# Attention with one reciprocal per group, its output and residual placed inside the next group's first pair, and the raw context copied by ScalarE

## The chip, the cores and the metric

The kernel runs on one core of a Trainium2 chip. The metric is the device time of one execution in microseconds (us). A core has TensorE (PE), VectorE (DVE), ScalarE (ACT), GpSimd (POOL) and SyncE (SP), which issues most of the DMAs. PSUM has eight banks of 128x512 f32.

## The reference

A decoder block on 32 sequences of 128 tokens with 128 features, in three stages with a layer norm behind each:

```
x = layernorm(x + mixer(x))              # a state-space scan
x = layernorm(x + attention(x, ctx))     # 16 heads of 8, mask, softmax, output weights
x = layernorm(x + experts(x))            # 16 experts, top 4, one shared expert
```

The change is in the second stage:

```
q, k, v = heads(x @ Wq + bq), heads(ctx @ Wk + bk), heads(ctx @ Wv + bv)
scores  = where(mask, -1e15, q @ k.T / sqrt(8))
attn    = softmax(scores);  out = (attn @ v) @ Wo + bo
```

## The kernel before, in words

`build` runs `mixer`, `attention` and `experts` one behind the other, each a block in which every engine has its own program, ordered against the others by semaphores. All sequences stand in SBUF as `x1` and `x2`.

`attention` (L949) works on eight groups of four sequences (`GS`, `NG`). The function `ahead` (L100) runs the same group function on each engine: a loop of two iterations of two groups, then four groups unrolled, whose argument `left` says how many groups follow. In group g the kernel finishes attention for g, takes the maxima of the scores for g+1, and makes q, k and v for g+2. Each sequence b of four is handled in two pairs p; a pair covers two banks.

- PE's `both(g, b, p)` (L1355) makes the transposed scores of g (`scoresT`, banks TT0 and TT1, read by ACT's exponentials at L1126) and the plain scores of g+1 (`scores`, banks SS0 and SS1, read by DVE's `maxima`, the reductions at L1211). Each `scores` waits until the reductions of the pair before have freed its banks. Both begin with the mask's product (L1328) and go on with the products at L1338. The first `scores` of a group waits in `stacked` (L1318) for `q_stack` and `k_stack` of g+1, first half.
- q and k of g+2 come from f32 products (`k_proj`, `q_proj`, L243), are split into three bf16 parts (ACT L208 and L214, DVE `part_rest` L221, POOL `part_third` L228), stored by SP to DRAM (`store_parts`, L253 and L256) and read back as stacks in two halves (`stack_k` L266, `stack_q` L275). `x1T` (L234) transposes x1 for q; DVE makes its low part at L201.
- The maxima of g+1 are split into bf16 parts by DVE (`split_maxima`, L1220 to L1226), transposed by PE (`max_rows`, L1387), copied by ACT (`store_max`, L1134), sent through DRAM (L1138) and laid under the q stack (`stack_max`, L1145). `scoresT` of a sequence waits for it.
- `weigh(b, 0)` (L1377) multiplies the probabilities with v, `weigh(b, 1)` with ones, so that the second half of the bank holds each head's row sum, already spread over the head's eight rows. DVE's `norm(b)` (L1228) takes the reciprocal of the 128x128 sums and multiplies, once for each sequence; the banks U0 and U1 alternate.
- `output(g)` (L1391) multiplies the four contexts with Wo into U0, and `residual_dve` (L114) adds `xb` (x1 and the bias, made by POOL at L1080) and takes the statistics for the layer norm; `normalise_pool` (L130) ends it on POOL.

The order on each engine is written out by hand. PE: pair 0 of sequence 0, k's product, the transposes of x1, pair 1, sequence 1 with q's product behind it, and so on; at the end `weigh(3, 1)`, v's product, `max_rows`, `output`. DVE: the reductions of sequence 0, x1's low part and k's rest, those of sequence 1, the split, q's rest, the others with `norm` between them, v, the residual. The last groups (`left` 1 and 0) hold the first steps of the experts' stage; POOL loads the experts' weights in the group with `left` 2 (L1523 and on).

Of the kernel before, what the change touches and what calls it, by code (L numbers as in the profile page):

```python
# [23 lines left out]
P = 128  # L24
# [924 lines left out]
def attention(nc, t, d, psum, a, e):  # L949
# [12 lines left out]
    with ExitStack() as ctx:  # L962
# [12 lines left out]
        ones_d = sb("ones_d", [P, UNITS * DIAG])  # L975
# [10 lines left out]
        recip = sb("recip", [P, 2, P])  # L986
# [13 lines left out]
        v_v, v_norm, v_max = sem("v_ready", GS), sem("ctx_norm", 2 * GS), sem("max_ready", 4 * GS)  # L1000
# [3 lines left out]
        p_mt, p_o = sem("max_mm", 2), sem("out_b_mm")  # L1004
# [16 lines left out]
        def _(sp):  # L1021
# [21 lines left out]
            def group(g, par, left):  # L1043
                if left == 3:
                    loads(g + 3, 1 - par)
# [14 lines left out]
        def _(pool):  # L1060
# [17 lines left out]
            def group(g, par, left):  # L1078
                pool.wait_ge(v_res.sem, v_res.at(g - 1, 0))
                pool.tensor_tensor(xb[:, :, :], x1[:, bass.ds(g * GS, GS), :], bc(b_o[:, None, :], [P, GS, P]), ALU.add)\  # L1080
                    .then_inc(g_x.sem, 1)
                if left >= 2:
                    masks(g + 2, par, (0,))
                    part_third(pool, a, g + 2, 1)
                    masks(g + 2, par, (1,))
                    part_third(pool, a, g + 2, 0)
                    masks(g + 2, par, (2, 3))
                if left == 3:
                    context_lo(g + 3, 1 - par)
# [15 lines left out]
            pool.memset(ones_d[:, :], 0.0).then_inc(g_init, 1)  # L1105
            normalise_pool(pool, NG - 1, t["x1_res"], x1_out, res, mv, rstd, norm_c, x1[:, NSEQ - GS:, :])
            pool.wait_ge(g_init, 6)
            pool.memset(ones_d[:, :].rearrange("p (i c) -> p i c", i=UNITS)[:, :, 0:P]
                        .rearrange("p i (c e) -> p i c e", e=4 * XD)[:, :, :, 0:XD], 1.0).then_inc(g_init, 1)
# [4 lines left out]
            prepare_pool(pool, e, prob[:, 0, 0:2, :, :].rearrange("p u i (x y) -> p (u i) x y", x=2))  # L1114
            ahead(pool, group)

        @block.scalar
        def _(act):
            for s in (a_exp, a_mt, *d_m, *d_ms, e.a_x, e.a_l, e.a_c):
                s.prime(act)  # L1120
# [27 lines left out]

            def group(g, par, left):
# [20 lines left out]
                exps(g, 2, 1)  # L1170
                if left:
# [5 lines left out]
                if left == 3:  # L1177
                    context_hi(act, a, g + 3, 1 - par)
# [13 lines left out]
        def _(dve):  # L1192
# [35 lines left out]
            def norm(g, b):  # L1228

                bank = (U0, U1)[b % 2]  # L1230
                dve.wait_ge(p_u.sem, p_u.at(g, b))
                dve.reciprocal(recip[:, b % 2, :], bank[:, P:2 * P]).then_inc(v_norm.sem, 1)  # L1232
                dve.wait_ge(v_norm.sem, v_norm.at(g, 2 * b))
                dve.wait_ge(p_o.sem, p_o.at(g - 1))
                dve.tensor_tensor(ctxT[:, b, :], bank[:, 0:P], recip[:, b % 2, :], ALU.mult).then_inc(v_norm.sem, 1)

            def group(g, par, left):
                if left:
                    maxima(g + 1, 0)
                if left >= 2:  # L1240
                    x1T_lo(dve, a, g + 2, PO)
                    part_rest(dve, a, g + 2, 1, PF)
                if left:
# [4 lines left out]
                if not left:  # L1248

                    dve.wait_ge(e.steps, PREPARED)  # L1250
                    x2T_lo(dve, e, 0, 0)
                if left:
                    maxima(g + 1, 2, (0, 1))
                norm(g, 0)
                if not left:
                    expert_scores(dve, e, 0)
                    rank_groups(dve, e, 0)
                if left:
                    maxima(g + 1, 2, (2, 3))
                    maxima(g + 1, 3, (0, 1))  # L1260
                norm(g, 1)
                if not left:
# [664 lines left out]
```

## Time and profile before

| what | us |
|---|---|
| median of 3 runs | 716.78 (712.73 to 718.43) |
| profiled execution | 715.72 |
| its span, first to last instruction | 713.9 |
| attention, about | 280 to 506 of the span |

How to read it: a row of a timeline is the start, the busy time of the merged instructions, the engine (q behind it: its sequencer, which issues DMAs), the line, the operation, out<-in, shapes and the number of instructions; in brackets the idle time of the engine just before and what ended it. Busy shares are means over stages with different limits.

### The profile page before, as it was taken

How to read it: one execution, taken by the hardware profiler on the slowest of the kernel's cores; microseconds unless marked ns; L12 is line 12 of the kernel's file. 1: busy time of each engine (PE TensorE's matmuls, PEld its weight loads, DVE VectorE, ACT ScalarE, POOL GpSimd, SP SyncE). 2: the span in 40 equal slices, each digit the busy share in tenths (PEclk: the TensorE clock that was granted, in tenths of full speed). 3: DMA queues.
4: the chain of work that ended last, by engine and by line, in shares of the span. 5: the costliest groups of instructions: out<-in, count | busy, mean ns of one | idle time of the engine just before them, and what ended most of it. 6: DMA issues, size and time to landing. Idle time of an engine off the chain costs nothing. (4 is left out here: it accounts for less than half of the span.)

```text
span 713.9 us, 17982 instructions
## 1 busy us (share of the span) xinstructions
PE 617.0 (86%) x6336; PEld 506.1 (71%) x6336; DVE 513.1 (72%) x1294; ACT 247.1 (35%) x428; POOL 259.7 (36%) x299
## 2 busy tenths in 40 slices
PE   6599999999998744978789879589799999999995
PEld 5468778778776532766567667467688888888884
DVE  3877887797785634778588888375477778787873
ACT  2453343354342301534436544234222222222221
POOL 4353854665564374342334435602101101110111
PEclk9989999999999955889799999688799999999998
DMA  6010000000000773276383565500000000000000
GB/s 200 5 56 2 15 15 15 0 15 15 0 16 1 172 165 67 82 131 149 80 180 117 120 140 144 120 7 4 30 1 30 30 0 29 29 0 29 16 16 16
DMA packets 53552, 40.32 MB, mean 56 GB/s; under 512 B 3968, under 2 KB 48288, under 8 KB 53488
## 3 DMA queue, kind: packets, MB, share of 16 engines
q1 hardware_dynamic: 50896, 36.74, 21.3%
q0 software_dynamic: 704, 1.92, 1.2%
q10 hardware_dynamic: 1888, 0.79, 0.5%
q8 instruction: 43, 0.70, 0.4%
q14 instruction: 21, 0.17, 0.1%
HBM read 24.10 MB, written 11.93 MB: 50 GB/s over the span
## 5 line engine op out<-in xcount | busy, mean ns | idle before, releaser
L1211 DVE TENSOR_REDUCE nmax<-bank 128x4 f32<-128x512 f32 x128 | 82.2, 684 | 56.2 <-PE bank L1338 55.9
L1824 PE MATMUL bank<-xT_hl_c,w_up 128*128 128x512 f32 x432 | 119.5, 413 | 1.9 <-ACTq L67 1.9
L133 POOL TENSOR_TENSOR rstd<-mv,norm_c 128x4 f32<-128x4 f32 x24 | 6.7, 281 | 306.7 <-DVE mv L127 285.9
L1126 ACT ACTIVATE prob<-bank 128x512 f32<-128x512 f32 x128 | 69.6, 596 | 99.7 <-PE bank L1338 87.2
L1328 PE MATMUL bank<-neg_i,mask 64*128 64x256 bf16 x512 | 58.4, 311 | 35.6 <-DVE nmax L1211 12.5
L1824 PEld LDWEIGHTS bank<-xT_hl_c,w_up 128*128 128x128 f32 x432 | 77.6, 193 | 15.7 <-ACTq L67 2.4
L1746 ACT ACTIVATE sg<-bank 128x512 f32<-128x512 f32 x72 | 43.1, 599 | 107.0 <-PE bank L1824 106.6
L1840 PEld LDWEIGHTS bank<-w_down,hid 128*128 128x128 f32 x576 | 74.4, 191 | 5.9 <-issue 0.6
L726 POOL TENSOR_TENSOR ramp<-upto,dec_hl 128x512 fp32r<-128x512 f32 x64 | 67.0, 1074 | 26.1 <-PE bank L856 26.1
L1840 PE MATMUL bank<-w_down,hid 128*128 128x128 f32 x576 | 75.6, 275 | 0.0
L1779 DVE TENSOR_TENSOR gu<-sg,bank 128x512 f32<-128x512 f32 x64 | 43.9, 685 | 21.8 <-PE bank L1824 10.3
L1328 PEld LDWEIGHTS bank<-neg_i,mask 64*128 64x128 bf16 x512 | 17.7, 101 | 53.9 <-issue 26.4
L1783 DVE TENSOR_TENSOR hid<-gu,bank 128x512 f32<-128x512 f32 x64 | 44.0, 688 | 6.5
L864 PE MATMUL bank<-w_x,xhl 128*128 128x256 f32 x192 | 42.2, 329 | 0.0
L1377 PE MATMUL bank<-prob,v_d 128*32 128x128 f32 x1024 | 38.6, 297 | 0.2 <-ACT prob L1126 0.2
L409 PE MATMUL bank<-xhl,w_feat 128*128 128x512 f32 (+1 forms) x96 | 30.2, 451 | 5.1 <-DVE b_rot L760 4.0
L1377 PE MATMUL bank<-prob,ones_d 128*32 128x128 f32 x1024 | 34.5, 275 | 0.0
L1232 DVE RECIPROCAL recip<-bank 128x128 f32<-128x128 f32 x32 | 30.4, 949 | 5.4 <-PE bank L1377 5.3
L864 PEld LDWEIGHTS bank<-w_x,xhl 128*128 128x128 f32 x192 | 29.5, 190 | 6.1 <-issue 5.3
L876 PE MATMUL bank<-c_rot,b_rot 128*128 128x256 f32 x128 | 32.9, 378 | 0.0
L1377 PEld LDWEIGHTS bank<-prob,v_d 128*32 128x32 f32 x1024 | 29.2, 118 | 4.2 <-issue 0.8
L1338 PE MATMUL bank<-k_stack,q_stack 48*128 48x128 bf16 x512 | 30.4, 248 | 0.0
(223 smaller groups left out, 1246.1 us busy)
## 6 DMA issues: line engine op xcount, KB each, us to landing
q_stack<-q_scratch SPq DMA_DIRECT2D x32, 192.0 KB, 5.3
k_scratch<-k_part SPq DMA_DIRECT2D x8, 384.0 KB, 2.6
q_scratch<-q_part SPq DMA_DIRECT2D x8, 384.0 KB, 2.9
k_stack<-k_scratch SPq DMA_DIRECT2D x32, 96.0 KB
x<-xT_in SPq DMA_DIRECT2D x8, 256.0 KB, 7.8
mask<-mask_in SPq DMA_DIRECT2D x8, 256.0 KB, 6.2
xres<-x_in SPq DMA_DIRECT2D x8, 256.0 KB, 2.8
q_scratch<-q_part SPq DMA_DIRECT2D x8, 256.0 KB, 3.1
```

Source lines behind the costliest of these rows:

```text
L726: pool.tensor_tensor(ramp[:, b % 2, v, :, :], bc(upto[:, None, :], [P, HEADS, P]), bc(dec_hl[:, v, bass.ds(g * GS + b, 1), :].rearrange("p ...
L864: mm = pe.matmul(PX[:, shift * D_INNER:(shift + 1) * D_INNER], xhl[:, par, a, b, 1 - shift:P + 1 - shift], w_x[:, v, :], start=(n == 0), s ...
L876: mm = pe.matmul(PG[:, 2 * k * P:(2 * k + 2) * P], b_rot[:, par, k, tok], c_rot[:, par, k, :, tok], start=False, stop=True, skip_group_che ...
L1126: act.activation(prob[:, b % 2, ORDER[n], :, :], (TT0, TT1)[n % 2][:, :], ACT.Exp, scale=XD ** -0.5)\
L1211: dve.tensor_reduce(nmax[:, b, 4 * u:4 * u + 4], (SS0, SS1)[n % 2][:, :].rearrange("p (i k) -> p i k", i=4), AX_X, ALU.max, negate=True).t ...
L1328: pe.matmul(banks[j][:, :].rearrange("p (i h k) -> p i h k", i=4, h=2)[:, :, half, :], mask[rows, par, b, kind + ver, :], bc(neg_i[rows, N ...
L1377: mm = pe.matmul(bank[32 * u:32 * u + 32, k * P:(k + 1) * P], src[:, i * P + 32 * u:i * P + 32 * u + 32], prob[:, b % 2, u, i, :], start=( ...
L1746: act.activation(sg[:, k, :], GG[k][:, :], ACT.Silu).then_inc(a_s.sem, 1)
L1779: dve.tensor_tensor(dst, sg[:, k, :], UU[k][:, :], ALU.mult).then_inc(v_gu.sem, 1)
L1783: dve.tensor_tensor(hid[:, c, :], gu[:, k, :], WW[(c - 1) % 2][:, :], ALU.mult).then_inc(v_hid.sem, 1)
L1824: mm = pe.matmul(bank[:, :], w_up[:, which, a, c, :], xT_hl[par][:, v, :], start=(n == 0), stop=(n == 2))
L1840: mm = pe.matmul(PO[:, b * P:(b + 1) * P], hid[:, c, b * P:(b + 1) * P], w_down[:, c, :], start=(c == 0 and b == 0), stop=(c == NC - 1), s ...
```

## The change

One reciprocal for a group: `weigh(b, 1)` multiplies with a sparse matrix `ones_s`, so that the sums of all four sequences fall on different rows of one 128x128 tile in U1. DVE's `invert` takes its reciprocal. PE's `spread_sums` brings the rows back over the heads by four f32 products with `pick_s`, into all of U1. The context of four sequences stands in U0; ACT's `context` copies it raw to SBUF, and DVE's `norm` multiplies the 128x512 at once. The output goes to U1.

The order: the first pair of g+1 stands ahead of `spread_sums(g)`, k's product and x1's transposes for g+3 and the second pair of g+1 ahead of `output(g)`. DVE has the reductions of g+2 and x1's low part and k's rest for g+3 ahead of the residual of g. v's product comes two products earlier. POOL's normalisation of g comes behind `head(g+1)`. ACT makes the context's first half for g+3 earlier. The loop of `ahead` has `left` 4 instead of 3.

```diff
@@ ahead
-        group(2 * i, 0, 3)
-        group(2 * i + 1, 1, 3)
+        group(2 * i, 0, 4)
+        group(2 * i + 1, 1, 4)
@@ POOL
-            def group(g, par, left):
+            def biased(g):
                 pool.wait_ge(v_res.sem, v_res.at(g - 1, 0))
                 pool.tensor_tensor(xb[:, :, :], x1[:, bass.ds(g * GS, GS), :], bc(b_o[:, None, :], [P, GS, P]), ALU.add)\
                     .then_inc(g_x.sem, 1)
+
+            def head(g, par, left):
                 if left >= 2:
                     masks(g + 2, par, (0,))
                     part_third(pool, a, g + 2, 1)
+
+            def group(g, par, left):
+                if left >= 2:
                     masks(g + 2, par, (1,))
                     part_third(pool, a, g + 2, 0)
+                if left >= 3:
+                    context_lo(g + 3, 1 - par)
+                if left >= 2:
                     masks(g + 2, par, (2, 3))
...
                 if left:
+                    head(g + 1, 1 - par, left - 1)
                     normalise_pool(pool, g, v_res, g_out, res, mv, rstd, norm_c, x2[:, bass.ds(g * GS, GS), :])
+                    biased(g + 1)
...
+            pool.affine_select(out=ones_s[:, :, :, :], in_=ones_s[:, :, :, :], compare_op=ALU.not_equal, fill=1.0, base=0,
+                               pattern=[[1, GS * UNITS], [0, 2], [-1, 16]], channel_multiplier=0).then_inc(g_init, 1)
+            for b in range(GS):
+                pool.affine_select(out=pick_s[:, b, :].rearrange("p (u i e) -> p u i e", u=UNITS, i=4),
...
@@ ACT
+            def context(g):
+                act.wait_ge(p_c.sem, p_c.at(g))
+                act.wait_ge(p_o.sem, p_o.at(g - 1))
+                act.activation(ctxT[:, :, :].rearrange("p b t -> p (b t)"), U0[:, :], ACT.Copy).then_inc(a_ctx.sem, 1)
...
                 exps(g, 2, 1)
+                if left >= 3:
+                    context_hi(act, a, g + 3, 1 - par)
                 if left:
                     store_max(g + 1, 1 - par, 0)
                 exps(g, 3, 0)
                 exps(g, 3, 1)
                 if left:
                     stack_max(g + 1, 1 - par, 0)
-                if left == 3:
-                    context_hi(act, a, g + 3, 1 - par)
+                context(g)
                 if left:
                     store_max(g + 1, 1 - par, 1)
@@ DVE
+            def invert(g):
+                dve.wait_ge(p_u.sem, p_u.at(g, GS - 1))
+                dve.reciprocal(recip[:, :], U1[:, 0:P]).then_inc(v_norm.sem, 1)
+
+            def norm(g):
+                dve.wait_ge(p_b.sem, p_b.at(g))
+                dve.wait_ge(a_ctx.sem, a_ctx.at(g))
+                flat = ctxT[:, :, :].rearrange("p b t -> p (b t)")
+                dve.tensor_tensor(flat, flat, U1[:, :], ALU.mult).then_inc(v_norm.sem, 1)
+
+            def head_parts(g, left):
                 if left >= 2:
                     x1T_lo(dve, a, g + 2, PO)
                     part_rest(dve, a, g + 2, 1, PF)
...
                 if left:
-                    maxima(g + 1, 3, (2, 3))
+                    maxima(g + 1, 2)
+                    maxima(g + 1, 3)
                     split_maxima(g + 1, 1)
-                norm(g, 2)
-                norm(g, 3)
                 if left >= 2:
                     values(g + 2, par)
+                invert(g)
+                if left >= 2:
+                    maxima(g + 2, 0, (0, 1))
+                norm(g)
+                if left >= 2:
+                    maxima(g + 2, 0, (2, 3))
+                    head_parts(g + 1, left - 1)
                 dve.wait_ge(p_o.sem, p_o.at(g))
                 dve.wait_ge(g_x.sem, g_x.at(g))
-                residual_dve(dve, g, U0, xb[:, :, :], g_out, v_res, dve_passed, res, stats, mv)
+                residual_dve(dve, g, U1, xb[:, :, :], g_out, v_res, dve_passed, res, stats, mv)
@@ PE
+            def spread_sums(g):
+                pe.wait_ge(v_norm.sem, v_norm.at(g, 0))
+                for b in range(GS):
+                    mm = pe.matmul(U1[:, b * P:(b + 1) * P], pick_s[:, b, :], recip[:, :], start=True, stop=True)
+                mm.then_inc(p_b.sem, 1)
...
                 weigh(g, par, 2, 1)
+                if left >= 2:
+                    values(g + 2, par)
                 weigh(g, par, 3, 0)
                 weigh(g, par, 3, 1)
-                if left >= 2:
-                    values(g + 2, par)
                 if left:
                     max_rows(g + 1, 1, (a_mt.sem, a_mt.at(g + 1, 0)))
+                    both(g + 1, 1 - par, 0, left - 1, 0)
+                spread_sums(g)
+                if left:
+                    head_parts(g + 1, 1 - par, left - 1)
+                    both(g + 1, 1 - par, 0, left - 1, 1)
                 output(g)
```

## Rows read from the trace of the kernel before

**Rows 1.** The page: busy time of the engines, and the group of the reciprocals
```profile
PE 617.0 (86%) x6336; PEld 506.1 (71%) x6336; DVE 513.1 (72%) x1294; ACT 247.1 (35%) x428; POOL 259.7 (36%) x299
...
L1232 DVE RECIPROCAL recip<-bank 128x128 f32<-128x128 f32 x32 | 30.4, 949 | 5.4 <-PE bank L1377 5.3
```

**Rows 2.** Busy time by stretch: one group, residual to residual
```profile
core 0: us, PE busy (x) PEld busy (x) DVE busy (x) ACT busy (x) POOL busy (x), PEclk, DMA share, GB/s
395.36:421.13 25.77, 22.75 (x480) 18.21 (x478) 21.74 (x48) 12.65 (x24) 10.41 (x12) 0.93 0.65 146
```

**Rows 3.** Timeline of PE, 395 to 422 us
```profile
395.87 0.63 PE L1328 MATMUL bank<-neg_i,mask 64*128 64x256 bf16 x4
...
396.86 1.65 PE L243 MATMUL bank<-c_hl,wqk_hl 128*128 128x512 f32 x3
...
399.59 0.38 PE L1328 MATMUL bank<-neg_i,mask 64*128 64x256 bf16 x4
...
401.02 0.40 PE L1328 MATMUL bank<-neg_i,mask 64*128 64x256 bf16 x4 [0.82 <-ACT prob L1126]
...
404.59 0.96 PE L243 MATMUL bank<-xT_hl,wqk_hl 128*128 128x512 f32 x3
...
417.73 0.29 PE L1387 MATMUL bank<-ident,npart 128*48 128x128 bf16 x2
419.94 1.16 PE L1394 MATMUL bank<-w_o,ctxT 128*128 128x128 f32 x8 [1.92 <-DVE ctxT L1235]
...
421.48 0.38 PE L1328 MATMUL bank<-neg_i,mask 64*128 64x256 bf16 x4
```

**Rows 4.** Timeline of PE at the ends of other groups
```profile
310.08 0.57 PE L1328 MATMUL bank<-neg_i,mask 64*128 64x256 bf16 x4
...
342.12 0.61 PE L1328 MATMUL bank<-neg_i,mask 64*128 64x256 bf16 x4 [4.52 <-issue]
...
454.07 0.61 PE L1328 MATMUL bank<-neg_i,mask 64*128 64x256 bf16 x4 [3.32 <-issue]
...
477.11 1.82 PE L1394 MATMUL bank<-w_o,ctxT 128*128 128x128 f32 x8 [2.02 <-DVE ctxT L1235]
...
481.07 0.61 PE L1328 MATMUL bank<-neg_i,mask 64*128 64x256 bf16 x4 [1.17 <-ACT prob L1126]
...
502.09 2.08 PE L1394 MATMUL bank<-w_o,ctxT 128*128 128x128 f32 x8 [3.07 <-DVE ctxT L1235]
```

**Rows 5.** Timeline of DVE, 395 to 417 us; last, L1224's durations, ns min/median/max
```profile
395.36 0.69 DVE L119 SCALAR_TENSOR_TENSOR res<-xb,bank 128x512 f32<-128x512 f32 x1 [0.46 <-PE bank L1394]
...
397.45 1.29 DVE L1211 TENSOR_REDUCE nmax<-bank 128x4 f32<-128x512 f32 x2
400.24 1.29 DVE L1211 TENSOR_REDUCE nmax<-bank 128x4 f32<-128x512 f32 x2 [1.50 <-PE bank L1338]
...
406.79 0.74 DVE L221 SCALAR_TENSOR_TENSOR rest<-bank,bqk,q_part 128x512 f32<-128x512 f32 x1
...
416.13 1.14 DVE L1224 CAST npart<-nrest 128x32 bf16<-128x32 f32 x1
...
L1224 DVE CAST npart<-nrest x16: 181/182/1178, 266.9 to 474.3; 128x32 bf16<-128x32 f32 x16
```

**Rows 6.** Timelines of ACT and POOL, 400 to 437 us
```profile
400.76 0.60 ACT L191 ACTIVATE xT_hl<-bank 128x512 fp32r<-128x512 f32 x1
...
408.83 1.16 POOL L228 TENSOR_TENSOR q_part<-rest,q_part 128x512 bf16<-128x512 f32 x1 [3.59 <-ACT q_part L214]
...
415.91 1.32 POOL L1075 TENSOR_TENSOR c_hl<-cin,c_hl 128x512 fp32r<-128x512 f32 x1 [1.59 <-ACT c_hl L185]
...
435.10 1.16 POOL L228 TENSOR_TENSOR q_part<-rest,q_part 128x512 bf16<-128x512 f32 x1 [3.82 <-ACT q_part L214]
```

**Rows 7.** One issue of L275 (ns, start), its landing, the page's issue row
```profile
L275 SPq DMA_DIRECT2D q_stack<-q_scratch x1: 554/554/554, 415.5 to 415.5; - x1
...
DMA to landing us min/median/max: 5.6/5.6/5.6
...
q_stack<-q_scratch SPq DMA_DIRECT2D x32, 192.0 KB, 5.3
```

More of the change, by code:

```diff
@@ L974, in attention @@
         zeros = sb("zeros", [P, P])
[L975 removed]
+        ones_s = sb("ones_s", [P, GS * UNITS, 2, 16])
+        pick_s = sb("pick_s", [P, GS, P])
         mask8 = a.mask8
@@ L1114, in _ @@
             prepare_pool(pool, e, prob[:, 0, 0:2, :, :].rearrange("p u i (x y) -> p (u i) x y", x=2))
+            biased(0)
+            head(0, 0, 4)
             ahead(pool, group)
@@ L1118, in _ @@
         def _(act):
-            for s in (a_exp, a_mt, *d_m, *d_ms, e.a_x, e.a_l, e.a_c):
+            for s in (a_exp, a_mt, a_ctx, *d_m, *d_ms, e.a_x, e.a_l, e.a_c):
                 s.prime(act)
@@ L1170, in group @@
                 exps(g, 2, 1)
+                if left >= 3:
+                    context_hi(act, a, g + 3, 1 - par)
                 if left:
@@ L1226, in split_maxima @@
                 dve.tensor_tensor(part(2), of(nrest), part(1), ALU.subtract).then_inc(v_split.sem, 1)
[L1228 to L1239, printed above, removed]
+            def invert(g):
[7 more added lines that the diff above has]
+            def head_parts(g, left):
                 if left >= 2:
@@ L1242, in group @@
                     part_rest(dve, a, g + 2, 1, PF)
+            def group(g, par, left):
+                if not left:
+                    dve.wait_ge(e.steps, PREPARED)
+                    x2T_lo(dve, e, 0, 0)
                 if left:
@@ L1248, in group @@
                 if not left:
[L1250 to L1255, printed above, removed]
                     expert_scores(dve, e, 0)
                     rank_groups(dve, e, 0)
[L1258 to L1262, printed above, removed]
                     select_experts(dve, e, 0)
@@ L1286, in _ @@
             dve.wait_ge(x1_out.sem, x1_out.at(NG - 1, 3))
+            maxima(1, 0)
+            head_parts(0, 4)
             ahead(dve, group)
@@ L1290, in _ @@
         def _(pe):
-            for s in (p_v, p_s, p_t, p_u, p_mt, p_o, e.p_x, e.p_l, e.p_c, e.p_u, e.p_w):
+            for s in (p_v, p_s, p_t, p_u, p_c, p_mt, p_o, p_b, e.p_x, e.p_l, e.p_c, e.p_u, e.p_w):
                 s.prime(pe)
@@ L1391, in output, with head_parts @@
             def output(g):
-                pe.wait_ge(v_norm.sem, v_norm.at(g, 7))
+                pe.wait_ge(v_norm.sem, v_norm.at(g, 1))
                 for b in range(GS):
-                    mm = pe.matmul(U0[:, b * P:(b + 1) * P], ctxT[:, b, :], w_o[:, :], start=True, stop=True)
+                    mm = pe.matmul(U1[:, b * P:(b + 1) * P], ctxT[:, b, :], w_o[:, :], start=True, stop=True)
                 mm.then_inc(p_o.sem, 1)
-            def group(g, par, left):
-                both(g, par, 0, left, 0)
+            def head_parts(g, par, left):
                 if left >= 2:
@@ L1401, in group @@
                     x1T(g + 2, par)
-                both(g, par, 0, left, 1)
+            def group(g, par, left):
                 if not left:
@@ L1450, in _ @@
             max_rows(0, 1, (a_mt.sem, a_mt.at(0, 0)))
-            pe.wait_ge(g_init, 7)
+            pe.wait_ge(g_init, 11)
             pe.wait_ge(v_v.sem, v_v.at(1, GS - 1))
+            both(0, 0, 0, 4, 0)
+            head_parts(0, 0, 4)
+            both(0, 0, 0, 4, 1)
             ahead(pe, group)
```

36 lines of the change are left out of this document (21 added, 15 removed).

## The prediction

> **What bounds the kernel now.** I read the page first, then the busy time by stretch, then the timelines of one group on each engine, SyncE's included. The page shows TensorE (PE) busy for 86% of the span, but this is a mean over three stages [rows 1]. The change touches only the attention stage, eight groups of four sequences between about 280 and 506 us. Seen by stretch, a group there lasts 25.77 us: PE is busy for 22.75 of them, VectorE (DVE) for 21.74, ScalarE (ACT) for 12.65, GpSimd (POOL) for 10.41, the DMA engines for 65% [rows 2]. None is full, so the time is in loops that pass from engine to engine. There are two.
>
> The first is seen on PE. At a group's end its last product, of the maxima, starts at 417.73; PE then idles for 1.92 us until DVE has the last context, makes the output at 419.94 (1.16 us), and only then begins the next group [rows 3]. This is what the change is aimed at.
>
> The second is seen only if one follows SyncE. The scores of group g+1 that PE makes at the head of group g (I call that moment S: 395.87 in this group, 421.48 in the next [rows 3]) need k_stack and q_stack, which come through DRAM. Their last link starts with POOL's third part of q at 408.83, 12.96 us after S; it ends at 409.99 [rows 6]. SyncE then issues the stores and the stacks of the first half; the last issue starts at 415.5 and lands 5.6 us later, at 421.1 [rows 7]. S of the next group is 421.48: 0.4 us of slack. So the DMA loop, S to third part (13.0), third part (1.2), to the landing (11.1), is 25.2 us long, and the group is hardly longer. Taking work out of the other loop only brings PE to a wait for the stacks.
>
> **The change, part by part.** *Reciprocals.* Four of 0.949 us a group become one [rows 1]. The four products of 128x128 become one of 128x512 out of PSUM; the nearest row of that size is the residual's, 0.69 [rows 5]. DVE loses 2.8 us, and a little more on the products. All of these stand behind the q part in DVE's order, where PE runs on from 404.59 to 418.0 with its own work [rows 3]; on the path this is worth nothing, on either side.
>
> *Products that spread the reciprocal.* Four f32 products of 128x128 a group are the form of the output: 1.16 us, and 1.82 with the clock at its lower level [rows 3, 4]. The 64 row-sum products stay 64, of the same shape, with another left side: zero. *ScalarE's copy* is 0.6 us by the row of the same shape [rows 6]; ACT is busy half of the time, and it stands behind the last exponentials: zero, or 0.6 if it delayed the copy of the maxima. The context's first half for g+3, moved ahead of the maxima's store on ACT, can delay that store by as much; the landing of the stacks comes later, so zero. *New waits.* PE waits for the one reciprocal, with k's product, the transposes and the second pair queued behind it; but PE will have stood at the stacks for longer than the 0.95 that it takes: zero, or 0.3 where the stacks are early (0.95 and its start, against 1.0 of pair). DVE's product waits for the spread and for ACT's copy, with the next two reductions queued behind; it is counted in the move below. The masks' new place on POOL and the loads, which only get one more unrolled case, cost nothing either. The constants (five selects instead of one fill) fall in POOL's idle time ahead of the first group: zero.
>
> *The move.* The first pair of g+1 now comes ahead of the spread products, and k's product, the transposes of x1 and the second pair ahead of the output. PE would be at the first pair at 418.0 and at its scores half a microsecond later, but the stacks land at 421.1: an idle time of 2.6 us takes the place of 1.92. From then on all hangs on the length from S to q's third part. Before, DVE after S = 395.87: the rest of the residual block until 397.45, a pair of reductions (1.2), idle until 400.24, a pair, x1's low part and k's rest, the second block's pairs, the split of the maxima, q's rest at 406.79, 10.92 after S [rows 5]. After, on DVE:
> - from the first scores to the first reduction 0.65 (scores at 399.59, reductions at 400.24 [rows 3, 5]), a pair 1.2: 1.9; the product 0.69: 2.6.
> - PE meanwhile: scores 0.55, spread 1.16 to 1.82, k's product 0.96 to 1.65, the transposes 0.45 to 0.85, transposed scores 0.45 (the 0.45 and 0.55 are the steps of its timeline [rows 3]): the second scores start 3.5 to 5.0 after S. Reductions start at 4.15 to 5.65, end 1.2 later.
> - x1's low part and k's rest, 0.65 and 0.7, then the whole residual block, 2.09 (395.36 to 397.45 [rows 5]): 8.8 to 10.3. Before, only 1.58 of it stood behind S, and beside PE's first products.
> - a pair of reductions for the second block 1.25, again 0.65 from PE's next scores to their reductions, a pair 1.25, the split 0.8: q's rest starts at 12.8 to 14.3.
> This is 1.9 to 3.4 later than 10.92. Which end: after an idle time of this kind PE worked at half clock over k's product (1.65 against 0.96 [rows 3]), so I lean to the long end, and take 2.9; S to third part becomes 15.9. Ends: 14.7, and 17.9 (next paragraph).
>
> *A cost in the shared access to SBUF.* One cast of the maxima took 1.14 us, not the 0.18 of most, while POOL subtracted c_hl beside it (415.91, 1.32 us) [rows 5, 6]. The change puts POOL's normalisation and bias, some 4.7 us behind the residual, beside the next split of the maxima, which lies in the loop. One such stretch is 1.0 us, two are 2.0. My 2.9 holds none in full; with two it is 4.9, which sets the upper end, 17.9. The Trainium skill states the mechanism (SBUF — State Buffer, section "SBUF: two separate sides"): DVE and GpSimd take turns at one pair of ports, held for a whole instruction, and a DVE instruction with two SBUF inputs counts as well as a fast copy. By the rule all four instructions of the split are open to it, by the row only the second cast; the trace agrees for that cast.
>
> *The stall at the loop's end.* PE idles for 4.52 us ahead of 342.12, once, where its loop of two groups jumps back, with nothing that it waits for [rows 4]. Before, it holds S back. After, it comes behind the output: the stacks have long been used, and DVE has k's rest and the residual to do. Of the 4.5 us I count 1.5 in the loop (the scores of the second block come that much after DVE is free), 0 and 4.5 being the ends. The Trainium skill (Runtime: NRT & Kernel Launch, section "Instruction fetch mechanics") says that a taken branch out of the pages held waits for code by DMA; the trace fits, and by it the stall stays one and only changes its place.
>
> **The sum.** Five lengths between S of 310.08 and the last one, 454.07, are 144.0 us [rows 4]. Each is 15.9 to the third part, 1.16 for it, and 10.8 to the landing (11.1 here; with the page's median landing of 5.3 in place of 5.6 it is 10.8 [rows 7]), and 0.1. The last is longer, since the experts' weights load beside it: 454.07 less 436.26, the end of POOL's part, is 17.8 in place of 10.9 [rows 4, 6]. So 5 x 17.06 + 4 x 10.9 + 17.8 + 1.5 = 148.2, and 4.2 us more than before; the stall that S no longer waits for (4.5) is already in it. Behind 454.07 come the output and the spread of two groups: 1.8 + 1.8 + 1.2 more on PE, less the waits of 2.02 and 1.17 and some 1.2 of short waits for DVE that this work fills [rows 4]: +0.4. At the very end the chain is one reciprocal, spread, product and output where the 3.07 of wait stood [rows 4]: equal. In all +4.6: 715.72 of the profiled execution (span 713.9) becomes 720.3. The median of the runs is 716.78, 1.1 above it, so I predict 721.5.
>
> **Rivals.**
> 1. *The gain as meant.* The stacks land early enough. Then a group loses 1.92 and the 0.82 at 401.02, and gains 1.16: 1.6 less, six times, and 2.5 of the loop stall: -12, so 704.8 (716.8 less 12, as for the next two). For it: the wait of 1.92 is real and PE works at full clock through the rest. Against it: the slack of 0.4 us at 421.1. It would need landings 2.5 us sooner.
> 2. *Only the loop stall goes.* If DVE's idle times (1.50 ahead of 400.24, and others [rows 5]) swallow product and residual, the loop keeps its length: -4.5 + 0.4, so 712.7. Against it: I could not place the residual anywhere but ahead of the reductions for which PE's scores wait.
> 3. *Slower.* The split is caught by POOL's normalisation in each group and the clock stays low through the head: S to third part is 17.9, 5 x 2.0 more than forecast, so 731.5. It decides from 16.4 on, where the sum passes +1%. For it: the 1.14 of the cast. Against: POOL may be through in time, and in the group shown the first split met nothing.
>
> **How the numbers follow.** About 1% (7 us) is what a measurement of this kernel can tell from no change. Forecast 0.53 (its own range 715 to 728), rival 1 0.15, rival 2 0.12, rival 3 0.20. Faster by over 1% (under 709.6): nearly all of rival 1, 0.15. Slower by over 1% (over 723.9): rival 3 and the upper part of the forecast, 0.30. Within: 0.55. The range 708 to 730 leaves out about 0.1 at each end.
>
> **What would show it.** PE's wait for DVE's context gone; in its place an idle time of 2 to 3 us ahead of the first scores (half a pair into the group), released by the DMA of q_stack; q's third part 15 to 17 us behind them, not 13; groups of 27 to 28 us where they had 25.5; DVE busy for 18.4 us in each; the loop stall behind an output. The prediction is wrong if a group lasts under 25.5 us, if the stacks land before PE asks, or if the residual does not hold up the second block's reductions.

## Result and profile after the change

The changed kernel takes 729.17 us (median of 4 runs, 725.74 to 732.13) against 714.75 for the kernel before beside it: a ratio of 1.0191 [1.0148, 1.0234]. The time lies inside the predicted range, but the change is slower by 1.9% where 0.7% was forecast. The profiled execution took 732.13 us with a span of 730.4, against 715.72 and 713.9: 16.5 us more in the span.

The page of the kernel after: busy times and the reductions' group (busy, mean ns | idle before, releaser); then one row of its view of waits (total us, times, longest).

```profile
PE 624.3 (85%) x6400; PEld 511.7 (70%) x6400; DVE 498.9 (68%) x1246; ACT 251.8 (34%) x436; POOL 261.5 (36%) x303
...
L1234 DVE TENSOR_REDUCE nmax<-bank 128x4 f32<-128x512 f32 x128 | 82.3, 684 | 81.5 <-PE bank L1363 81.1
```
```profile
PE bank L1353 <- DVE nmax L1234: 25.7, 14, 2.8
```

DVE does 14.2 us less than in [rows 1], as the change means it to. But ahead of the reductions it now idles for 81.5 us (56.2 before), waiting for PE's scores, while PE waits 25.7 us for the reductions. Before, PE's wait for the reductions was 12.5 us. The two engines wait for each other: they are links of one loop.

Busy time by stretch, one group of the kernel after, residual to residual:

```profile
380.33:410.31 29.98, 23.71 (x494) 18.85 (x490) 19.32 (x43) 13.10 (x26) 10.40 (x12) 0.94 0.58 124
```

A group lasts 30 us instead of the 25.77 of [rows 2], at nearly the same mean granted clock (0.94 against 0.93) and with less work on DVE. The prediction had looked for 27 to 28 us, with 18.4 us of DVE. Next PE in the group that answers to [rows 3]:

```profile
400.16 0.39 PE L1353 MATMUL bank<-neg_i,mask 64*128 64x256 bf16 x4 [0.72 <-DMA q_stack<-max_scratch]
...
402.75 0.39 PE L1353 MATMUL bank<-neg_i,mask 64*128 64x256 bf16 x4 [1.98 <-DMA q_stack<-q_scratch]
...
403.30 1.16 PE L1418 MATMUL bank<-recip,pick_s 128*128 128x128 f32 x8
...
406.51 1.16 PE L1433 MATMUL bank<-w_o,ctxT 128*128 128x128 f32 x8
408.67 0.40 PE L1353 MATMUL bank<-neg_i,mask 64*128 64x256 bf16 x4 [1.00 <-ACT prob L1143]
...
413.75 0.39 PE L1353 MATMUL bank<-neg_i,mask 64*128 64x256 bf16 x4 [2.45 <-DVE nmax L1234]
```

The wait for DVE's context is gone: the output at 406.51 starts without one. In its place stand 0.72 us for the maxima under the stack and 1.98 for the stack of q, together 2.7 where 2.6 were forecast, and 2.45 for the reductions behind the residual. DVE in the same group, beside [rows 5]:

```profile
403.48 1.29 DVE L1234 TENSOR_REDUCE nmax<-bank 128x4 f32<-128x512 f32 x2 [2.46 <-PE bank L1363]
...
406.61 1.29 DVE L1234 TENSOR_REDUCE nmax<-bank 128x4 f32<-128x512 f32 x2 [1.25 <-PE bank L1363]
409.05 0.69 DVE L201 TENSOR_TENSOR xT_hl<-bank,xT_hl 128x512 fp32r<-128x512 f32 x1 [1.15 <-ACT xT_hl L191]
...
410.31 0.68 DVE L119 SCALAR_TENSOR_TENSOR res<-xb,bank 128x512 f32<-128x512 f32 x1
...
412.40 1.29 DVE L1234 TENSOR_REDUCE nmax<-bank 128x4 f32<-128x512 f32 x2
...
415.72 0.32 DVE L1243 CAST npart<-nmax 128x32 bf16<-128x32 f32 x1
416.08 1.21 DVE L1245 TENSOR_TENSOR nrest<-nmax,npart 128x32 f32<-128x32 f32 x1
417.32 0.51 DVE L1247 CAST npart<-nrest 128x32 bf16<-128x32 f32 x1
...
417.97 0.74 DVE L221 SCALAR_TENSOR_TENSOR rest<-bank,bqk,q_part 128x512 f32<-128x512 f32 x1
```

Read from S = 402.75: second reductions at S + 3.9, residual at 7.6, second block at 9.7, q's rest at 15.2. Before, q's rest came at S + 10.9. The next lines are of ACT and POOL, beside [rows 6], then SyncE's issue of q's first stack, and the time to landing (us) of these issues, beside [rows 7]:

```profile
405.88 1.46 ACTq L1162 DMA_DIRECT2D q_stack<-max_scratch  x2
407.44 1.09 ACT L1143 ACTIVATE prob<-bank 128x512 f32<-128x512 f32 x2 [5.55 <-issue]
...
419.24 0.63 ACT L214 ACTIVATE q_part<-rest 128x512 bf16<-128x512 f32 x1
```
```profile
414.97 1.04 POOL L140 TENSOR_TENSOR x<-res,rstd 128x512 f32 x1 [0.17 <-POOL rstd L136]
415.96 1.27 POOL L1082 TENSOR_TENSOR xb<-x,b_o 128x512 f32<-128x512 f32 x1
417.18 0.61 POOL L1072 CAST mask<-mask 128x512 bf16<-128x512 uint8 x1
419.94 1.16 POOL L228 TENSOR_TENSOR q_part<-rest,q_part 128x512 bf16<-128x512 f32 x1 [2.15 <-ACT q_part L214]
```
```profile
427.76 0.82 SPq L275 DMA_DIRECT2D q_stack<-q_scratch  x2
...
DMA to landing us min/median/max: 3.4/3.9/4.3
```

q's third part starts at 419.94, 17.2 behind S. The next S is 432.55. At each of the first four S's PE waits for the stack of q (0.46, 1.72, 0.49 and 1.98 us); at 432.55 it is idle for 2.75 with no releaser in the profile. So in the changed kernel the loop through DRAM sets the period, as the prediction said; it is only longer.

Two things are to be seen. The first is that three of DVE's four short operations of the split, from 415.72 on, are stretched beside POOL's operations from 414.97 to 417.8, and they end where one of POOL's ends. The second is that ACT stands idle for 5.55 us ahead of its exponentials. Ahead of them in its order is L1162, the issue that puts the maxima under the stack, which waits until they are in DRAM. Before, the same issue (L1145) did not hold the exponentials up; they waited for PE:

```profile
397.64 1.45 ACTq L1145 DMA_DIRECT2D q_stack<-max_scratch  x2
399.79 1.08 ACT L1126 ACTIVATE prob<-bank 128x512 f32<-128x512 f32 x2 [2.60 <-PE bank L1338]
```

The loop can be taken apart for every kernel from the timelines of PE and POOL. "To third part" is the sum of the five spans from S to the start of q's third part, "to S" the four from its end to the next S, "last" the same beside the loading of the experts' weights. With 5 x 1.16 for the third parts they add up to the last column, from the first S to the sixth. These are sums of one profiled execution each, and an execution can lie 5 us and more off its kernel's median. The ratios come from all runs, each against the kernel before as it ran beside them: its median was 714.06 us beside e1 to e4, 714.64 beside e5 to e8 and 716.59 beside e9 to e12, so across these sets ratios are compared and not times. Runs that fell in a slower state of the chip (one of e4, two of e7, one of e10) are left out of the ratios, e4's time is the median of its other three, and e4 has no line because its profiled execution was the disturbed one.

| kernel | to third part | to S | last | sum | ratio to before |
|---|---|---|---|---|---|
| before | 68.2 | 52.2 | 17.8 | 144.0 | 1 |
| forecast | 81.0 | 43.6 | 17.8 | 148.2 | 1.007 |
| after | 92.0 | 44.9 | 18.1 | 160.8 | 1.0191 |
| e1 reciprocal part alone | 63.0 | 62.6 | 18.9 | 150.2 | 1.0059 |
| e2 order alone | 87.6 | 42.8 | 17.6 | 153.8 | 1.0176 |
| e3 POOL later | 91.6 | 45.2 | 13.5 | 156.1 | 1.0150 |
| e5 and statistics later | 78.8 | 45.6 | 14.5 | 144.8 | 0.9993 |
| e6 and exponentials first | 73.3 | 46.1 | 14.8 | 140.0 | 0.9874 |
| e7 k first, alone | 93.0 | 37.9 | 16.7 | 153.3 | 1.0049 |
| e8 all four | 69.6 | 43.1 | 14.8 | 133.3 | 0.9830 |
| e9 DVE work in the loop | 78.2 | 52.6 | 19.1 | 155.7 | 1.0171 |
| e10 the same behind it | 71.5 | 56.2 | 15.4 | 148.9 | 1.0028 |
| e11 before, k first | 65.3 | 50.3 | 18.2 | 139.6 | 0.9879 |
| e12 e8 with four reciprocals | 68.6 | 45.4 | 14.2 | 134.0 | 0.9828 |

One more thing differs between these executions: TensorE's granted clock at the head of the groups, which the mean of a whole group hides. In the 6 us from S on it was 0.50, 0.72, 1.00, 1.00 and 0.50 of full speed in the five groups of the kernel after. The spans from S to q's third part in the same order are 19.2, 18.8, 17.9, 17.2 and 18.9. The fives of other kernels are: e3 1.00, 0.51, 0.50, 1.00, 0.51; e5 0.50, 0.72, 1.00, 1.00, 1.00; e6 0.51, 0.72, 1.00, 0.72, 1.00; e8 and e12 1.00 in all. Of the kernels in the new order, the groups with the full 1.00 alone have these means from S to the third part: after 17.6 (two groups), e3 18.0 (two), e5 15.4 (three), e6 13.1 (two), e8 13.1 (four, without the group of the loop's jump, 17.2).

### The profile page after: what moved, and what is told of

Its sections match the earlier page's. It is cut to its first block and busy times, and to the rows that moved or that the text cites. A ratio compares the mean times of both kernels' runs of the same rounds, so it can differ in the third digit from the quotient of the medians.

```text
span 730.4 us, 18042 instructions
## 1 busy us (share of the span) xinstructions
PE 624.3 (85%) x6400; PEld 511.7 (70%) x6400; DVE 498.9 (68%) x1246; ACT 251.8 (34%) x436; POOL 261.5 (36%) x303
## 3 DMA queue, kind: packets, MB, share of 16 engines
q0 software_dynamic: 704, 1.92, 1.1%
## 5 line engine op out<-in xcount | busy, mean ns | idle before, releaser
L1234 DVE TENSOR_REDUCE nmax<-bank 128x4 f32<-128x512 f32 x128 | 82.3, 684 | 81.5 <-PE bank L1363 81.1
L1353 PE MATMUL bank<-neg_i,mask 64*128 64x256 bf16 x512 | 56.9, 304 | 56.8 <-DVE nmax L1234 25.7
L1793 ACT ACTIVATE sg<-bank 128x512 f32<-128x512 f32 x72 | 43.1, 599 | 106.7 <-PE bank L1871 105.1
L1353 PEld LDWEIGHTS bank<-neg_i,mask 64*128 64x128 bf16 x512 | 17.8, 100 | 75.5 <-issue 37.1
L1826 DVE TENSOR_TENSOR gu<-sg,bank 128x512 f32<-128x512 f32 x64 | 43.8, 685 | 21.7 <-PE bank L1871 10.2
L1072 POOL CAST mask<-mask 128x512 bf16<-128x512 uint8 x32 | 19.2, 612 | 69.6 <-PE bank L1363 69.1
L1402 PE MATMUL bank<-prob,ones_s 128*32 128x128 f32 x1024 | 38.2, 295 | 0.0
L1406 PE MATMUL bank<-prob,v_d 128*32 128x128 f32 x1024 | 36.5, 286 | 0.2 <-ACT prob L1143 0.2
L1402 PEld LDWEIGHTS bank<-prob,ones_s 128*32 128x32 f32 x1024 | 29.3, 118 | 5.5 <-issue 3.4
L1406 PEld LDWEIGHTS bank<-prob,v_d 128*32 128x32 f32 x1024 | 27.6, 114 | 4.2 <-ACT prob L1143 0.6
```

Source lines behind the costliest of these rows:

```text
L1234: dve.tensor_reduce(nmax[:, b, 4 * u:4 * u + 4], (SS0, SS1)[n % 2][:, :].rearrange("p (i k) -> p i k", i=4), AX_X, ALU.max, negate=True).t ...
L1353: pe.matmul(banks[j][:, :].rearrange("p (i h k) -> p i h k", i=4, h=2)[:, :, half, :], mask[rows, par, b, kind + ver, :], bc(neg_i[rows, N ...
L1402: mm = pe.matmul(U1[32 * u:32 * u + 32, 0:P], ones_s[:, 4 * b + i, :, :].rearrange("p r c -> p (r c)"), prob[:, b % 2, u, i, :], start=(b ...
L1406: mm = pe.matmul(U0[32 * u:32 * u + 32, b * P:(b + 1) * P], v_d[:, par, b, i * P + 32 * u:i * P + 32 * u + 32], prob[:, b % 2, u, i, :], s ...
L1793: act.activation(sg[:, k, :], GG[k][:, :], ACT.Silu).then_inc(a_s.sem, 1)
L1826: dve.tensor_tensor(dst, sg[:, k, :], UU[k][:, :], ALU.mult).then_inc(v_gu.sem, 1)
```

## Experiments

**e1 and e2: which part of the change costs?** e1 keeps the one reciprocal, the spread, the raw copy and the one product, and gives all engines the order of before. e2 keeps before's four reciprocals and takes the order of after.

```diff
 e1, against after (PE; the other engines alike)
                 if left:
                     max_rows(g + 1, 1, (a_mt.sem, a_mt.at(g + 1, 0)))
-                    both(g + 1, 1 - par, 0, left - 1, 0)
                 spread_sums(g)
-                if left:
-                    head_parts(g + 1, 1 - par, left - 1)
-                    both(g + 1, 1 - par, 0, left - 1, 1)
                 output(g)
 e2, against before (PE; the other engines alike)
                     max_rows(g + 1, 1, (a_mt.sem, a_mt.at(g + 1, 0)))
+                    both(g + 1, 1 - par, 0, left - 1, 0)
+                    head_parts(g + 1, 1 - par, left - 1)
+                    both(g + 1, 1 - par, 0, left - 1, 1)
                 output(g)
```

> The reciprocal part alone, in the order of before: one reciprocal, spread products, ACT's copy and one product a group, all behind the maxima of the group's end. Loop theory (the cost comes from what stands between a group's first scores and q's third part): nothing is added there, and at the group's end reciprocal 0.95, spread 1.16 and product 0.69 take the place of 1.92 of wait: 715, between 712 and 719. Rival A (the spread products and the chain of waits around the one reciprocal cost the time): 725 or more.

> The order alone, with before's four reciprocals: the first pair, k's product, x1's transposes and the second pair of g+1 ahead of the output of g. Loop theory: the residual block (2.1) and the stretched split (1.4) stand in the loop, only the product (0.7) does not, so most of the loss stays: 724 to 731. Rival A: 715 or less, since PE's wait of 1.92 a group is gone.

e1 took 717.65 us, 1.0059 [1.0015, 1.0104]; e2 726.27, 1.0176 [1.0130, 1.0223]. Both lie where the loop theory had them. The order alone carries nearly all of the loss. PE's timeline of e1 shows where its small loss is:

```profile
399.23 1.16 PE L1403 MATMUL bank<-recip,pick_s 128*128 128x128 f32 x8 [1.72 <-DVE recip L1246]
401.17 1.75 PE L1418 MATMUL bank<-w_o,ctxT 128*128 128x128 f32 x8 [0.78 <-DVE ctxT L1253]
```

In before's order the 1.92 of wait becomes 1.72 and 0.78 with the 1.16 of the spread between them, all ahead of S: "to S" grows by 10.4, and "to third part" shrinks by 5.2. (e1's profiled execution was its longest, 721.08.)

**e3: POOL's normalisation out of the way of the split.** The second mask and q's third part of g+3, together in a new function `second`, go ahead of the normalisation of g.

```diff
                     head(g + 1, 1 - par, left - 1)
+                    second(g + 1, 1 - par, left - 1)
                     normalise_pool(pool, g, v_res, g_out, res, mv, rstd, norm_c, x2[:, bass.ds(g * GS, GS), :])
                     biased(g + 1)
```

> The changed kernel, with POOL's normalisation of g and bias behind the second mask and q's third part of g+3, so that they no longer stand beside the first split of the maxima. Loop theory with the shared access: the split, 2.3 in place of 0.9 us, is short again, 1.4 less in each of five loops: 722, between 720 and 725. Rival B (the hold does not reach the path, the low clock of PE does): 729, as changed.

724.80 us, 1.0150 [1.0111, 1.0189]: 0.4% better than after, with intervals that overlap, at the edge of what was expected. DVE in e3, its split and q's rest, then ACT and POOL:

```profile
409.47 0.69 DVE L201 TENSOR_TENSOR xT_hl<-bank,xT_hl 128x512 fp32r<-128x512 f32 x1 [1.80 <-ACT xT_hl L191]
...
416.15 0.18 DVE L1247 CAST npart<-nmax 128x32 bf16<-128x32 f32 x1
416.36 0.19 DVE L1249 TENSOR_TENSOR nrest<-nmax,npart 128x32 f32<-128x32 f32 x1
...
417.01 0.75 DVE L221 SCALAR_TENSOR_TENSOR rest<-bank,bqk,q_part 128x512 f32<-128x512 f32 x1
```
```profile
418.81 1.09 ACT L1147 ACTIVATE prob<-bank 128x512 f32<-128x512 f32 x2 [1.90 <-PE bank L1367]
419.78 0.63 ACT L214 ACTIVATE q_part<-rest 128x512 bf16<-128x512 f32 x1
```
```profile
420.49 1.16 POOL L228 TENSOR_TENSOR q_part<-rest,q_part 128x512 bf16<-128x512 f32 x1 [7.19 <-ACT q_part L214]
```

The stretch is gone: 1.21 has become 0.19, so it was POOL's work that made it. It had been on the path: over the five groups q's rest starts on the mean 15.3 behind S in e3 and 16.5 in the kernel after. But the loop did not get shorter: 91.6 against 92.0. From q's rest to the third part it now takes 3.1 on the mean, where it took 1.9, because ACT makes q's second part only behind an exponential that waits 1.90 for PE. In the group shown x1's low part waits longer for ACT as well (1.80 for 1.15). S is 402.52 here, and the third part starts 18.0 behind it. What e3 gained in its profile is in the column "last", 13.5 for 18.1. POOL's timeline has a reason at hand: the first of the weights is issued behind the normalisation now, at 458.48, 5.7 us behind the end of the third part; in the kernel after it is issued at 456.72, 4.1 behind it. The stacks would then get ahead of more of the weights. This was not tried by itself, but all the kernels of the table agree with it: where the first weight is issued 4.1 to 4.7 us behind that end, "last" is 16.7 to 19.1, and where it is 5.7 to 5.9 (e3, e5, e6, e8, e10, e12), 13.5 to 15.4.

**e4: the exponentials ahead of ACT's wait.** ACT's issue of the maxima under the stack goes behind the second exponentials, x1's high part and k's first part.

```diff
-                stack_max(g, par, 1)
                 exps(g, 0, 1)
                 if left >= 2:
                     x1T_hi(act, a, g + 2, PO)
                     part_first(act, a, g + 2, par, 1, PF)
+                stack_max(g, par, 1)
```

> The changed kernel, with ACT's stacking of the maxima (which waits for their landing in DRAM) behind the second exponentials and x1's high part and k's first part. Loop theory: x1's low part on DVE no longer waits 1.15 us for ACT, five times: 724, between 722 and 727. Rival C (the maxima's landing is hidden behind the residual anyway): 729.

717.81 us, 1.0079 [1.0022, 1.0135]: 1.1% better than after, and more than the 722 to 727 expected, from the move of one wait on an engine that is busy for a third of the time. The intervals of the two do not overlap.

**e5 and e6: residual's statistics out of the loop, then e4's edit as well.** e5 is e3, and leaves only the sum of the residual ahead of the second block's reductions; `bn_stats` and `bn_aggr` come behind q's rest. DVE's new function `second` holds the second block's reductions, the split and q's rest. e6 is e5 with e4's edit.

```diff
-                residual_dve(dve, g, U1, xb[:, :, :], g_out, v_res, dve_passed, res, stats, mv)
+                residual_sum(dve, g, U1, xb[:, :, :], g_out, v_res, res)
+                if left:
+                    second(g + 1, left - 1)
+                residual_stats(dve, g, v_res, dve_passed, res, stats, mv)
```

> As e3, and on DVE only the residual's sum (0.69) stays ahead of the second block's reductions; its statistics (1.4) go behind q's rest. Loop theory: 1.4 less in each of five loops than e3 (724.8): 718, between 716 and 721. Rival B (PE's low clock and its own work set the length): no less than 723.

> As e5, and ACT's stacking of the maxima behind the second exponentials, as in e4. Loop theory: the gains of e3, e4 and the statistics add, since all three lie in one chain: 711, between 708 and 715. Rival: they overlap (one hides another) and it stays at 717 or above.

e5 took 714.30 us, 0.9993 [0.9947, 1.0038]; e6 706.02, 0.9874 [0.9812, 0.9935]. Both gained more than expected (716 to 721, and 708 to 715). Putting 1.4 us of DVE's work behind q's rest shortened "to third part" by 12.8 in five groups, 2.6 in each, and by as much in the groups at full clock (18.0 to 15.4): more than its length. DVE's timelines show both halves of it: q's rest starts 1.5 sooner, and ACT no longer has a late exponential ahead of q's second part, which takes off another 1.1. e4's edit on top of it takes the groups at full clock from 15.4 to 13.1: x1's low part waited up to 2.99 for ACT in e5 and does not in e6. So ACT's wait for the maxima lay in the loop.

**e7: SyncE issues the stack of k ahead of q's stores.** The link from q's third part to the landing is SyncE's: three stores of q, then six issues for k, then q's two. k is stored long before.

```diff
                     store_parts(sp, a, g + 2, par, 1)
-                    store_parts(sp, a, g + 2, par, 0)
-                    for half in range(2):
-                        stacks(g + 2, par, half)
+                    k_half(g + 2, par, 0)
+                    store_q(g + 2, par)
+                    q_half(g + 2, par, 0)
+                    k_half(g + 2, par, 1)
+                    q_half(g + 2, par, 1)
```

> The changed kernel with one edit on SyncE: the six issues of k's stack, first half (2.75 us), go ahead of the stores of q instead of behind them; no engine's work changes. Loop theory: from q's third part to the landing of q's stack 9 us instead of 11.2, five times: 719, between 716 and 723. Rival D (the landing of the stacks only coincides with the wait, PE and DVE set the length): 729.

718.48 us, 1.0049 [1.0000, 1.0098], 1.4% better than after, with intervals that do not overlap, and as expected. No engine's work changed, so in the changed kernel the landing of the stacks does set S. "To S" fell from 44.9 to 37.9, from 11.2 to 9.5 for one group; "to third part" stayed. SyncE in e7, last store of q to q's first stack:

```profile
387.81 1.60 SPq L1043 DMA_DIRECT2D q_scratch<-q_part  x3
...
391.74 0.84 SPq L275 DMA_DIRECT2D q_stack<-q_scratch  x2
```

q's stack is issued 3.9 us after the first store of q. In the kernel after it is 6.6:

```profile
421.13 2.73 SPq L256 DMA_DIRECT2D q_scratch<-q_part  x3
423.98 3.73 SPq L266 DMA_DIRECT2D k_stack<-k_scratch  x6
```

**e8: all four edits, e6 and e7 together.**

> e6 and e7 together. Loop theory: the loop through the stacks falls below PE's own work of some 23 us a group, so that PE becomes the bound and the gain is smaller than the sum: 704, between 700 and 709, under both kernels. Rival: the loop was already left behind in e6, and nothing is gained on it.

701.09 us, 0.9830 [0.9768, 0.9892]: faster than both kernels, 3.5% under after (0.9830 / 1.0191). Against e6 the intervals overlap, so these runs do not show that e7's edit still gains anything on top of e6, where PE at a group's end mostly waits for the maxima and not for q. PE in one group of e8, and DVE:

```profile
361.78 0.40 PE L1400 MATMUL bank<-neg_i,mask 64*128 64x256 bf16 x4 [0.51 <-DMA q_stack<-q_scratch]
...
376.17 0.39 PE L1400 MATMUL bank<-neg_i,mask 64*128 64x256 bf16 x4 [1.04 <-DVE nmax L1275]
...
385.87 0.39 PE L1400 MATMUL bank<-neg_i,mask 64*128 64x256 bf16 x4 [0.65 <-DMA q_stack<-max_scratch]
...
386.32 0.38 PE L1400 MATMUL bank<-neg_i,mask 64*128 64x256 bf16 x4
```
```profile
372.88 0.75 DVE L239 SCALAR_TENSOR_TENSOR rest<-bank,bqk,q_part 128x512 f32<-128x512 f32 x1
373.54 0.86 DVE L141 BATCH_NORM_STATS2 stats<-res 128x6 f32<-128x128 f32 x4
```

q's rest is at S + 11.1 again (361.78 to 372.88), as before the change, and the statistics stand behind it. The group is 24.5 us long, from 361.78 to 386.32, and at its end the stack of q no longer makes PE wait at 386.32: only 0.65 for the maxima is left. In these 24.5 us PE waits nowhere for much longer than 1 us.

**e9 and e10: the same DVE work ahead of q's rest and behind it.** Into the kernel before go three reductions of a 128x512 of zeros, 1.86 us, in each of the six groups that still make a q; in e9 ahead of the second block's reductions, in e10 behind q's rest.

```diff
 e9, against before
                     part_rest(dve, a, g + 2, 1, PF)
+                    added()
                 if left:
                     maxima(g + 1, 1)
 e10, against before
                     part_rest(dve, a, g + 2, 0, PF)
+                    added()
```

> The kernel before, with three more reductions of 128x512 on DVE in each group (2.05 us, on zeros, into a tile of their own), between k's rest and the second block's reductions, where the change put the residual. Loop theory: 2.05 more in each of five loops, less the slack at the stacks: 721 to 724. Rival E (DVE is idle for 4 of 25.8 us a group, the work fits in): 716 or less.

> The kernel before, with the same three reductions behind q's rest, outside the loop. Loop theory: they only push the later reductions, for which PE waits little: 715 to 718, clearly less than in e9. Rival E': DVE's sum decides and it costs as much as in e9.

e9 took 728.73 us, 1.0171 [1.0111, 1.0230]; e10 719.05, 1.0028 [0.9988, 1.0068]. In e9 the work and PE's wait behind it:

```profile
409.23 1.86 DVE L1231 TENSOR_REDUCE added_t<-zeros 128x4 f32<-128x512 f32 x3
```
```profile
412.34 0.39 PE L1334 MATMUL bank<-neg_i,mask 64*128 64x256 bf16 x4 [2.55 <-DVE nmax L1212]
```

Five times 1.86 is 9.3, and "to third part" grew by 10.0. The kernel as a whole got six times 1.86, 11.2, and grew by 12, which is more than the 721 to 724 expected. Behind q's rest the same work costs 2 us, at the upper end of what was expected, and the interval holds zero. So what decides is not whether DVE has idle time but on which side of q's rest the work stands. Which loop passes the cost on is not shown by this: in e9 PE waits for the reductions themselves, and at none of the S's from 310 to 433 does it wait for the stack of q. (e10's profiled execution was one of its longest, 725.38, so its row in the table is on the high side.)

**e11: e7's edit on the kernel before.**

> The kernel before, with the edit of e7 on SyncE. Theory of two loops: before, PE's own loop is almost as long as that of the stacks, so that 2 us less in the latter give little: 711, between 708 and 714, against 10 less in the changed kernel. Rival: the stacks' loop alone was the bound, and it gives as much as in e7, 705 or less.

710.62 us, 0.9879 [0.9793, 0.9964]. The time is the one expected. The ratio, though, is nearly that of e7 to after, 1.2% for 1.4%, where the theory of two loops had clearly less; the interval is wide, from 0.4 to 2.1%, and the two medians alone (710.62 and 716.59) make 0.8%. The profiled execution does not show the stacks as the bound before. PE's waits in it, from 305 to 456 us, and then those of the kernel before:

```profile
PE bank L1413 <- DVE ctxT L1254: 9.6, 6, 1.9
PE bank L1347 <- DMA q_stack<-max_scratch: 0.9, 1, 0.9
```
```profile
PE bank L1394 <- DVE ctxT L1235: 10.6, 6, 1.9
PE bank L1328 <- DMA q_stack<-max_scratch: 3.5, 1, 3.5
```

Neither has a wait for `q_stack<-q_scratch`. The third and fourth group last 25.1 and 24.5 us where they lasted 25.4 and 25.6, and the edit takes 1.9 from "to S", against 7.0 in the changed kernel. So before the change the two loops are nearly of one length, and the stacks are not shown to set the period.

**e12: e8 with before's four reciprocals.** e2 with the edits of e3 to e5 and e7.

> e8 with before's four reciprocals and products a group (no spread products, no copy on ACT). If the reciprocal part is worth nothing by itself: 701, as e8, between 698 and 705. If DVE's 3.3 us a group count once the loop is repaired: 710 or more. If the spread products (1.16 of PE a group) are the dearer: 696 or less.

705.51 us, 0.9828 [0.9772, 0.9884], the same ratio as e8's. (The time is 0.5 us over the 698 to 705 expected; the kernel before, too, was 2 us slower beside it than beside e8.) The one reciprocal neither gains nor costs anything that these intervals can show, not even where the loop is short.

## Why the prediction was right and where it was wrong

The time lies in the range, but one step of the sum was well too short, and a cost left to the upper end was there in every group.

- *Two loops, and the one through the stacks takes over*: right for the kernel after. The wait of 1.92 is gone and one of 1.98 for `q_stack` has come, and e7, which moves only SyncE's issues, gives 1.4% back. That this loop was the longer one already before is not shown (e9, e11).
- *Reciprocals are worth nothing*: right in size (e12 against e8, e2 against after). Alone, in the old order, the part costs 0.6% (e1): the spread and a second wait stand ahead of S there. The prediction had priced these products only as part of the move.
- *From the third part to the landing 10.9, the last 17.8*: right, 11.2 and 18.1; +1.6 of the miss.
- *S to third part 15.9*: this is the step that failed. It measured 18.4 as a mean of five (17.2 to 19.2), so 92.0 where 81.0 stood, and that is 11.0 of the 12.6 us by which the sum fell short. DVE's timeline says where: q's rest starts 16.5 behind S on the mean where 13.8 was forecast. These are the parts:
  - *Shared access to SBUF* was put at the upper end only. The split took 2.3 us on the mean (2.0 to 2.7 in the five groups) instead of the 0.8 of the sum, so about 1.5 of the missed 2.5 us a group are its stretch. The condition of rival 3 (over 16.4) was met in every group, its mechanism was at work in every group, and its 731.5 came nearest. But the stretch does not decide alone: e3 took it away and left "to third part" at 91.6, because ACT was late next. By the Trainium skill (SBUF — State Buffer, section "SBUF: two separate sides") all four instructions of the split are open to it, by the row of before only one cast. The trace of after agrees with the page: each of the four is stretched in one group or another, the difference of two SBUF operands to 1.21, the first cast to 1.08 in the first group, and in the second group these two:

```profile
356.73 1.03 DVE L1247 CAST npart<-nrest 128x32 bf16<-128x32 f32 x1
357.79 1.22 DVE L1249 TENSOR_TENSOR npart<-nrest,npart 128x32 bf16<-128x32 f32 x1
```

  - *The clock of the heads.* The prediction leaned to the long end for a low clock, and took 2.9. In the two groups whose head had the full 1.00, the second block's reductions start 10.2 and 9.7 behind S, as forecast (9.8), and only the split makes them late (17.9 and 17.2). In the three with a low clock they start at 10.9 to 11.5, and the third part at 18.8 to 19.2. Over all five that is another 0.8 us a group.
  - *The base was one group.* 12.96 is the second shortest of the five spans before: 15.2, 13.8, 12.5, 13.0, 13.6, on the mean 13.6. Counted from that mean, the step grew by 4.8 us a group where 2.9 was forecast, so 0.7 of the missed 2.5 was in the base already.
  - ACT's edits at zero, since "the landing of the stacks comes later": I priced what was added to ACT, and not that its exponentials for the next group now stand behind the landing of the maxima (5.55 idle), of which x1's high part and so DVE's low part (1.15) and PE's next scores (1.00) hang. No step of the sum held this. In the group shown it is covered by the long end taken for PE's head, but it is real time: moving the one wait gave 1.1% (e4).
  - "The whole residual block, 2.09" was counted at its own length. Its place is worth more: with 1.4 us of it gone, each group lost 2.6 (e5 against e3). DVE's reductions, PE's next scores and ACT's exponentials are one chain, and a delay is passed on.
- *Loop stall, 1.5 in the loop*: its row behind the output is there, shorter than the 4.52 of [rows 4]. What of it reached q's third part cannot be told, since the head of the same group also had a clock of 0.72. PE in the kernel after:

```profile
350.29 0.61 PE L1353 MATMUL bank<-neg_i,mask 64*128 64x256 bf16 x4 [2.17 <-issue]
```

- *Tail +0.4*: from the sixth S to the end it is 259.7 us (730.4 less 470.73), and 259.8 before (713.9 less 454.07), so nothing.

So the first to the sixth S is 16.8 longer, and that is the 16.5 us of the span. Not settled: why the clock of a head is low in one group and full in another, and whether it is the later issue of the weights that makes the last landing 3 to 4 us sooner in e3, e5, e6, e8 and e12.

## What to carry to other kernels

When an engine's share is far under full and its waits point at other engines, look for a loop and lay its links end to end, DMA issues included; here it ran over PE, DVE, ACT, POOL, SyncE and DRAM. Do it for every group and not for one, and check whether the loops before the change are of nearly one length. Work costs by its place: ahead of the last link of the loop it cost at least its length here (e5, e9), behind it next to nothing (e10), whatever the idle time of the engine says. Before moving work off one wait, look also for waits that stand in front of the loop's links on the idle engines: order alone, on ACT, SyncE, DVE and POOL, was worth 3.5% here, more than any arithmetic saved.

## What the runs showed of the hardware

- SyncE's issues cost the loop more than the last transfer: nine issues from 421.13 to 427.7, 6.6 us, stand ahead of q's stack in the kernel after, and the landing takes 3.4 to 4.3 us more. Their order alone was worth 1.4% in the changed kernel (e7).
- DVE's subtractions of two SBUF operands of 128x32 took up to 1.22 us beside POOL's work and 0.19 without it (e3); its casts of 128x32 in the kernel after from 0.32 to 1.08 against 0.18.
- PE's stall where the loop of two groups jumps back was 4.52 before and 2.17 after, and in e8 it is

```profile
340.82 0.40 PE L1400 MATMUL bank<-neg_i,mask 64*128 64x256 bf16 x4 [3.44 <-issue]
```

so it is not a fixed price; what sets it was not tried.
